# Moving transfers into neighbouring blocks, the projection into the int8 attention, and half of the value rounding to GpSimd

## What is computed

```python
def _layernorm(x, axis=-1, eps=1e-05):
    m = jnp.mean(x, axis=axis, keepdims=True)
    v = jnp.var(x, axis=axis, keepdims=True)
    return (x - m) / jnp.sqrt(v + eps)
...
def _L1_xattn_ref(x, cond, Wq, bq, Wkv, bkv, Wp, bp):   # H = 16 heads of hd = 32
    q = (x @ Wq + bq).reshape(1, B * N, H, hd)
    kv = (cond @ Wkv + bkv).reshape(1, -1, 2, H, hd)
    k, v = (kv[:, :, 0], kv[:, :, 1])
    ...
    q = _fq_sym(q, axis=-1)
    k = _fq_sym(k, axis=-1)
    v = _fq_sym(v, axis=2)
    attn = jnp.einsum('bhqd,bhkd->bhqk', q, k)
    attn = jax.nn.softmax(attn.astype(jnp.float32), axis=-1)
    attn = _fq_unsigned(attn, axis=-1)
    out = jnp.einsum('bhqk,bhkd->bhqd', attn, v)
    ...
    return out @ Wp + bp
```

## Time and profile before

| | us |
|---|---|
| median of three runs | 2641.4 (2641.16 to 2645.72) |
| profiled execution | 2642.37 |
| its span, first to last instruction | 2640.6 |
| granted TensorE clock, mean | 0.948 |

### The profile page before, as it was taken

How to read it: one execution, slowest core, us unless ns; L and a number is a source line. 1 busy time by engine, 2 the same in 40 slices (tenths; PEclk the granted TensorE clock), 3 DMA queues, 4 the chain that set the end, 5 groups by cost and what they waited for, 6 DMA issues and landing times. The chain is left out here.

```text
span 2640.6 us, 32466 instructions
## 1 busy us (share of the span) xinstructions
PE 2326.4 (88%) x11672; PEld 1586.5 (60%) x11672; DVE 1799.9 (68%) x3545; ACT 1252.7 (47%) x2207; POOL 503.7 (19%) x411
## 2 busy tenths in 40 slices
PE   3779999999999999967994988788888779999998
PEld 2556666666666665546772455545555437777776
DVE  7855777777777779776784966777777843464444
ACT  4443466666656666533442024676666853211111
POOL 7710033333333243420000011111101000000000
PEclk9879999999999999988997999999999969899999
DMA  3231100000010000024443000000000005456662
GB/s 133 107 135 36 36 17 29 8 29 28 13 32 9 29 9 13 0 80 183 168 144 137 0 21 10 1 10 1 6 5 1 1 20 196 180 219 230 224 226 75
DMA packets 47067, 184.89 MB, mean 70 GB/s; under 512 B 6272, under 2 KB 11136, under 8 KB 36672
## 3 DMA queue, kind: packets, MB, share of 16 engines
q1 hardware_dynamic: 46912, 182.86, 19.1%
HBM read 173.93 MB, written 8.91 MB: 69 GB/s over the span
## 5 line engine op out<-in xcount | busy, mean ns | idle before, releaser
L402 PE MATMUL wide_a<-wide_w,ctxT 128*128 128x256 f32 (+1 forms) x2048 | 436.1, 366 | 2.8 <-POOL wide_eps L371 2.8
L402 PEld LDWEIGHTS wide_a<-wide_w,ctxT 128*128 128x128 f32 x2048 | 367.0, 190 | 76.3 <-issue 35.7
L384 POOL TENSOR_TENSOR wide_sums<-wide_sums,wide_s 128x512 f32<-128x512 f32 x224 | 302.0, 1348 | 458.2 <-ACT wide_s L532 445.0
L1633 ACT ACTIVATE int_prob<-int_a,int_shift,int_qscale 128x512 uint8<-128x512 f32 x256 | 199.1, 786 | 103.5 <-PE int_a L1499 102.9
L427 PE MATMUL wide_scores<-wide_q,wide_keysT 128*128 128x512 f32 x512 | 238.4, 604 | 10.8 <-ACT wide_s L528 10.8
L437 PE MATMUL wide_o<-wide_s,wide_values 128*128 128x512 f32 x512 | 232.5, 597 | 3.5 <-ACT wide_s L532 3.5
L528 ACT COPY wide_s<-wide_scores 128x512 f32<-128x512 f32 x256 | 148.6, 586 | 180.0 <-PE wide_scores L427 168.6
L1753 DVE TENSOR_REDUCE int_peaks<-int_a 128x1 f32<-128x512 f32 x256 | 169.6, 685 | 60.0 <-PE int_a L1499 57.8
L1499 PE MATMUL int_a<-int_keys,int_qrows 96*128 96x512 bf16 x512 | 166.0, 408 | 41.8 <-DVE int_peaks L1753 34.8
L590 DVE TENSOR_TENSOR wide_top<-wide_top,wide_s 128x512 f32<-128x512 f32 x240 | 165.7, 691 | 15.4 <-ACT wide_s L528 9.6
L427 PEld LDWEIGHTS wide_scores<-wide_q,wide_keysT 128*128 128x128 f32 x512 | 87.9, 189 | 146.9 <-ACT wide_s L528 86.0
(11 more groups left out here) (416 smaller groups left out, 4277.1 us busy)
## 6 DMA issues: line engine op xcount, KB each, us to landing
moe_gate_up<-hbm_m_gu SPq DMA_DIRECT2D x34, 1408.0 KB, 6.2
moe_down<-hbm_m_down_a SPq DMA_DIRECT2D x34, 512.0 KB, 7.0
causal_wqkv<-hbm_wqkv SPq DMA_DIRECT2D x8, 1536.0 KB, 6.8
ctxT<-hbm_ctxT SPq DMA_DIRECT2D x4, 2048.0 KB, 14.8
oproj_raw<-hbm_wproj SPq DMA_DIRECT2D x8, 1024.0 KB, 5.3
ctxT_again<-hbm_ctxT SPq DMA_DIRECT2D x4, 2048.0 KB, 14.3
moe_down<-hbm_m_down_b SPq DMA_DIRECT2D x34, 192.0 KB, 7.3
wide_unit<-hbm_ffn_units SPq DMA_DIRECT2D x24, 256.0 KB, 2.6
```

The costliest lines, as they stand in the source:

```text
L384: ins = pool.tensor_tensor(sums[0][:, :], before, part[:, j, :], ALU.add)
L402: mm = pe.matmul(a[h][:, j, cols], ctxT[:, kc, t * P:(t + 1) * P], w[g % 2][:, kc, cols], start=(kc == 0), stop=(kc == KC - 1))
L1633: act.activation(prob[u % 4][:, j * 512:(j + 1) * 512], a[n % 4][:, :], ACT.Exp, bias=shift[:, u % NU:u % NU + 1], scale=qscale[:, t, h:h ...
```

## The change

- The layernorm before the FFN becomes part of the FFN's block (same instructions, without transposes and their copies), and `context_loads` are issued in that block.
- Two transfers of the causal stage and four of the decay stage move from the layernorm's block to the start of the next block. In the causal one they stand in front of the units' transfers in SyncE's queue.
- ScalarE takes one root of a constant ahead of the statistics in each layernorm, so the table is loaded then.
- The projection goes into the int8 stage. Its weights are loaded into the place of the query weights once the last values have been turned; TensorE runs its products right behind the last `finish`, those of the last chunk when VectorE has written its output; VectorE adds the bias ahead of the last `finish` and the products at the end.
- GpSimd rounds pieces 3 and 4 of each chunk, three instructions each; the pieces stand at steps 2, 6, 2 and 6. GpSimd now follows the common list, with its key instructions at their steps.
- In the last chunk VectorE casts six of eight turns of a head, before four.

```diff
@@ build_middle, ffn_stage, causal_attention_stage
-                    sp.dma_start(wqkv[1][:, :, :, :], A["wqkv0"][1]).then_inc(s_w[1], 16)
-                    sp.dma_start(wo[1][:, :, :], A["wo0"][1]).then_inc(s_wo[1], 16)
...
+                sp.dma_start(wqkv[1][:, :, :, :], A["wqkv0"][1]).then_inc(s_w[1], 16)
+                sp.dma_start(wo[1][:, :, :], A["wo0"][1]).then_inc(s_wo[1], 16)
                 for p in range(NP):
...
-            layernorm_stage(nc, "ln2", C, x, xT, xn=xn, loads=context_loads)
-            ffn_stage(nc, C, xn, weights, x)
+            ffn_stage(nc, C, x, weights, context_loads)
...
+            @block.sync
+            def _(sp):
+                loads(sp)
...
+                act.activation(std[:, NT:], eps[:, 0:1], ACT.Sqrt)
                 for t in range(NT):
...
+                    link(dve.bn_stats(stats[:, t, :], x[:, t, :]))
+                    dve.bn_aggr(mv[:, t, :], stats[:, t, :]).then_inc(s_var, 1)
+                for t in range(NT):
+                    dve.wait_ge(s_std, t + 1)
+                    link(dve.reciprocal(rstd[:, t:t + 1], std[:, t:t + 1]))
+                    link(dve.tensor_scalar(xn[:, t, :], x[:, t, :], mv[:, t, 0:1], rstd[:, t:t + 1], ALU.subtract, ALU.mult))
                     mx_dequantise(dve, link, xn[:, t, :], stat, power[:, :], shifted[:, :], deq[t][:, :]).then_inc(s_q, 1)
@@ int8_cross_attention_stage
-            return j % 2 == 0 and not (j % 4 == 2 and h % HC == HC - 1 and h // HC + 1 < CC)
+            if h // HC + 1 == CC:
+                return j % 4 != 3
+            return j % 2 == 0 and not (j % 4 == 2 and h % HC == HC - 1)
...
+                sp.wait_ge(s_b, use_b["value turned", CC - 1, 3] + 1)
+                sp.wait_ge(s_kp, CC * NS)
+                sp.dma_start(wp, A["x_wp"]).then_inc(s_wp, 16)
+                sp.dma_start(bp[:, :], A["x_bp"]).then_inc(s_wp, 16)
...
+                def round_values(c, piece):
+                    pool.wait_ge(s_vs, c + 1)
+                    cols = slice((piece - 1) * (SC // 4), piece * (SC // 4))
+                    if c >= 1:
+                        pool.wait_ge(s_b, use_b["value turned", c - 1, 3] + 1)
+                    pool.wait_ge(s_vc, c * NS + 2 * piece)
+                    link(pool.tensor_scalar(vT[:, cols], vT[:, cols], vstat[:, NS + 1:NS + 2], -127.0, ALU.mult, ALU.max))
+                    link(pool.tensor_scalar(vT[:, cols], vT[:, cols], ROUND_INT, ROUND_INT + 127.0, ALU.add, ALU.min))
+                    pool.tensor_scalar(vq[:, cols], vT[:, cols], ROUND_INT, None, ALU.subtract).then_inc(s_vp, 1)
+
+                for step in order:
+                    what, c, n = step
+                    if what == "key high":
+                        first_rest(c, n)
+                    elif what == "key middle":
+                        last_part(c, n)
+                    elif what == "value rounded" and n >= 3:
+                        round_values(c, n)
...
+                def project_out():
+                    pe.wait_ge(s_wp, 32)
...
+                    for c in range(CC):
+                        if c == CC - 1:
+                            pe.wait_ge(s_put, CC)
+                        for t in range(NT):
+                            mm = pe.matmul(a[t][:, :], outT[:, c, t * P:(t + 1) * P], wp[:, c, :], start=(c == 0), stop=(c == CC - 1))
...
+                        if x == CC - 1:
+                            dve.wait_ge(s_wp, 32)
+                            for t in range(NT):
+                                link(dve.tensor_tensor(residual[:, t, :], residual[:, t, :], bp[:, :], ALU.add))
                         finish(x)
...
+                    dve.wait_ge(s_xo, t + 1)
+                    dve.tensor_tensor(residual[:, t, :], residual[:, t, :], a[t][:, :], ALU.add)
@@ int8_order
-            place(base + max(4 * piece - 2, 0), "value rounded", c, piece)
+            place(base + (4 * ((piece - 1) % 2) + 2 if piece else 0), "value rounded", c, piece)
@@ build_last: of the loop over e the part for e = 1 moves into decay_attention_stage
+                sp.dma_start(wkv[1][:, :, :], A["d_wkv"][1]).then_inc(s_w[1], 16)
+                sp.dma_start(wq[1][:, :, :], A["d_wq"][1]).then_inc(s_w[1], 16)
+                sp.dma_start(decay[1][:, :, :, :], A["decay"][1]).then_inc(s_wo[1], 16)
+                sp.dma_start(wo[1][:, :, :], A["d_wo"][1]).then_inc(s_wo[1], 16)
```

More of the change, by code:

```diff
@@ L1040, in _, with ffn_stage @@
                     dve.tensor_tensor(x[:, t, :], x[:, t, :], acc[t][:, :], ALU.add)
-def ffn_stage(nc, C, xn, weights, x):
+def ffn_stage(nc, C, x, weights, loads):
     NF = 4
     with Stage(nc, "ffn") as st:
+        xn = st.sb("xn", [P, NT, DM])
+        stats = st.sb("stats", [P, NT, 6])
+        mv = st.sb("mv", [P, NT, 2])
+        eps = st.sb("eps", [P, 1])
+        std = st.sb("std", [P, NT + 1])
+        rstd = st.sb("rstd", [P, NT])
         deq = [st.sb(f"deq{e}", [P, DM]) for e in range(2)]
@@ L1087, in _ @@
             def _(act):
+                act.wait_ge(s_eps, 1)
+                act.activation(std[:, NT:], eps[:, 0:1], ACT.Sqrt)
+                for t in range(NT):
+                    act.wait_ge(s_var, t + 1)
+                    act.activation(std[:, t:t + 1], mv[:, t, 1:2], ACT.Sqrt, bias=eps[:, 0:1]).then_inc(s_std, 1)
                 for t in range(NT):
@@ L1468, in turn_values @@
                 def turn_values(c, m):
-                    pe.wait_ge(s_vq, 4 * c + m + 1)
+                    if m < 2:
+                        pe.wait_ge(s_vq, 2 * c + m + 1)
+                    else:
+                        pe.wait_ge(s_vp, 2 * c + m - 1)
                     e = use_b["value turned", c, m]
@@ L1568, in _ @@
                         finish(x)
+                project_out()
             @block.scalar
@@ L1738, in round_values @@
                         link(dve.tensor_scalar(s_v, peak_v, 1.0 / 127.0, 1e-8, ALU.mult, ALU.max))
-                        link(dve.reciprocal(inv_v, s_v))
+                        if c >= 1:
+                            dve.wait_ge(s_vp, 2 * c)
+                        dve.reciprocal(inv_v, s_v).then_inc(s_vs, 1)
+                        dve.wait_ge(s_vs, c + 1)
+                        return
+                    if piece >= 3:
                         return
@@ L1810, in _ @@
                     elif what == "finish":
+                        if x == CC - 1:
+                            dve.wait_ge(s_wp, 32)
+                            for t in range(NT):
+                                link(dve.tensor_tensor(residual[:, t, :], residual[:, t, :], bp[:, :], ALU.add))
                         finish(x)
-def projection_stage(nc, name, zT, n_in, w_dram, bias_dram, x):
-    with Stage(nc, name) as st:
-        w = st.sb("w", [P, n_in, DM])
-        bias = st.sb("bias", [P, DM])
-        acc = [st.ps(f"acc{t}", [P, DM]) for t in range(NT)]
-        s_in, s_mm, s_dve = (st.sem(n) for n in ("loaded", "products", "dve"))
-        with nc.Block() as block:
-            @block.sync
-            def _(sp):
-                sp.dma_start(w[:, :, :], w_dram).then_inc(s_in, 16)
-                sp.dma_start(bias[:, :], bias_dram).then_inc(s_in, 16)
-            @block.tensor
-            def _(pe):
-                pe.wait_ge(s_in, 32)
-                for t in range(NT):
-                    for j in range(n_in):
-                        mm = pe.matmul(acc[t][:, :], zT[:, j, t * P:(t + 1) * P], w[:, j, :], start=(j == 0), stop=(j == n_in - 1))
-                    mm.then_inc(s_mm, 1)
-            @block.vector
-            def _(dve):
-                link = Chain(dve, s_dve).after
-                dve.wait_ge(s_in, 32)
-                for t in range(NT):
-                    link(dve.tensor_tensor(x[:, t, :], x[:, t, :], bias[:, :], ALU.add))
-                    dve.wait_ge(s_mm, t + 1)
-                    link(dve.tensor_tensor(x[:, t, :], x[:, t, :], acc[t][:, :], ALU.add))
+                for t in range(NT):
+                    dve.wait_ge(s_xo, t + 1)
+                    dve.tensor_tensor(residual[:, t, :], residual[:, t, :], a[t][:, :], ALU.add)
 def build_int8_attention(nc, C, A, x, context):
```

64 lines of the change are left out of this document (35 added, 29 removed).

## The result

| kernel | median of its runs, us | ratio to before, 95% interval |
|---|---|---|
| before | 2641.9 (2641.16 to 2645.72) | |
| after | 2602.2 (2596.01 to 2610.53) | 0.985 (0.982 to 0.988) |

A forecast was written before the change was run, and what follows sets the result against it. Bound: a row of stages with all-engine barriers between; no engine full in int8 chunk 0. Sum from 2642.4: -17.5 - 0.4 - 7.5 + 9.6 + 6.4 + 0.5 = -8.9, 2633.5, forecast 2633 us; own range 2622 to 2636, eight in ten 2612 to 2652.

The forecast's parts named there:

- FFN's seam: Between causal stage and FFN: with the layernorm inside the FFN's block only SyncE waits for its 12.97 us issue; 17.5 us gained.
- Causal seam: Before the causal stage: two transfers moved to the next block shorten VectorE's wait; 0.4 us gained, bounds 0 and 0.9.
- Projection: After attention: 12 of 16 matmul passes run straight behind the last sums; 7.5 us gained after 0.3 for bias additions.
- six slow passes: In the projection after attention: six matmul passes at 0.85 us, as before, and six at 0.43, 7.7 us together.
- The pieces on GpSimd: Int8 stage, value rounding moved off VectorE: a loss of 9.6 us in chunks 0 to 2 and 6.4 in chunk 3.
- VectorE's way to SBUF: Int8 stage: GpSimd's instructions, 3.0 us each, block VectorE's SBUF access; about 10.8 us standing still in a chunk's first 25.
- my walk through the earlier trace: Chunk 0 with GpSimd and VectorE taking alternating turns: VectorE's piece instructions take 1.8 to 2.9 us, 10.8 us standing in all.
- a lock over the whole instruction: SBUF access: an exclusive lock held for the whole instruction by VectorE's two-port modes and its instructions with two SBUF inputs.
- The 45% passed on: Int8 stage: 45% of VectorE's 10.8 us standing lengthens a chunk, 4.8 us, bounds 0 and all of it.
- the 1.6 us for the pieces removed: Int8 stage: two pieces fewer on VectorE gain 0.6 and 1.0 us, 1.6 us a chunk.
- Casts in the last chunk: VectorE takes 24 of 32 casts instead of 16: middle nothing, near the end -1.9, after the exponentials +1.0; +0.5 us in all.
- the first, 2615: GpSimd is cheap, 1.05 to 1.5 us an instruction; int8 gain and loss cancel, only the seams count: 2615 us, chance 0.22.

The follow-up runs named there:

- 2591.0 us kernel: The changed kernel with the last chunk's casts as before and each piece of values rounded in two instructions instead of three, on both engines: 2591.0 us (0.981).

## Why the prediction was wrong, point by point

By the medians the 30.7 us between forecast and result divide so: 16.5 for a cost of the int8 stage that didn't come, some 9 that the int8 loop gained, by the experiments through the key order, which I had not costed, and 5.5 for the seams, which brought 30.9 where I had 25.4.

- **FFN's seam**, -17.5: right (-17.9 at the first reduction and -17.1 at the stage's end in the profile; 18.1 us earlier and 20.6 in the median where it was made alone). A further 2.6 us came ahead of the int8 loop at a higher clock, which I had not; 1.2 of them came also where nothing ahead was changed.
- **Causal seam**, -0.4: it can't be told. The end of that stage is 0.6 us earlier after, but 3.2 earlier in the kernel with the projection's merge alone, which changes nothing ahead of it, and between 7.0 earlier and 5.3 later in kernels that share the causal edit.
- **Projection**, -7.5: right in kind, low by 1.6 (-9.1), inside its bounds. I had six slow passes; there were about four, which is 0.8 of the 1.6. The bias additions, charged with 0.3, cost nothing: with the old casts the tail is 14.1 us with and without them.
- **The pieces on GpSimd**, +16.0: wrong. This is the step that failed: its size is off in both of its factors (1 and 2), and beside it an effect of the same rewritten loop was left out (3).
  1. *The step "VectorE's way to SBUF"*. GpSimd's instructions were longer than I assumed, 3.7, 3.8 and 2.9 us instead of 3.0:

```profile
L1419 POOL TENSOR_SCALAR int_vT<-int_vT,int_vstat x8: 3707/3712/4043, 1610.5 to 2043.4; 128x1024 f32<-128x1024 f32 x8
L1420 POOL TENSOR_SCALAR int_vT<-int_vT x8: 3636/3794/3962, 1614.3 to 2047.5; 128x1024 f32<-128x1024 f32 x8
L1421 POOL TENSOR_SCALAR int_vq<-int_vT x8: 2777/2870/3201, 1618.4 to 2051.3; 128x1024 bf16<-128x1024 f32 x8
```

     VectorE's lines beside them, of after, should by my walk through the earlier trace rows have shown 2 to 3.5 us, and show their usual 0.7 or at most 0.8 us more:

```profile
L1818 DVE TENSOR_SCALAR int_vT<-int_vT,int_vstat x8: 742/800/1352, 1615.2 to 2043.0; 128x1024 f32<-128x1024 f32 x8
L1819 DVE TENSOR_SCALAR int_vT<-int_vT x8: 693/694/1481, 1616.0 to 2043.9; 128x1024 f32<-128x1024 f32 x8
L1820 DVE TENSOR_SCALAR int_vq<-int_vT x8: 694/1401/1410, 1616.7 to 2045.4; 128x1024 bf16<-128x1024 f32 x8
```

     Adding up what every VectorE instruction took over its usual time, VectorE stood 3.2, 3.3, 2.0 and 2.0 us in chunks 0 to 3, not 10.8. Against that, the 1.4 us a chunk that it had stood before in steps 35 to 42 are gone. The earlier trace rows had misled me, since GpSimd's instructions there are 1.2 and 1.7 us long: one can't see in them whether VectorE waits for the end or for a part. The Trainium skill, "SBUF — State Buffer", section "Who interferes with whom", which I had cited for a lock over the whole instruction, doesn't fit these rows: VectorE's pieces took at most 0.8 us more beside GpSimd instructions of 2.8 to 4.0 us.
  2. *The 45% passed on, and the 1.6 us for the pieces removed.* With 2 x 2.13 us less work and 2 to 3.3 us of standing, VectorE is left with 1 to 2 us less a chunk, and steps 0 to 15 went from 122.2 us (all on VectorE, new key order) to 120.5. That difference is inside what such kernels differ by: seven of them with all pieces on VectorE at the same steps have 117.9 to 122.2. Its two halves are clearer: steps 0 to 11, where GpSimd works beside VectorE, took 4.6 us more (84.1 to 88.7) although one of VectorE's pieces left them, and steps 12 to 15, which lost their piece, 6.3 less (38.1 to 31.8). So both effects of the forecast are there, the loss far smaller and the gain larger. Where the standing was nearly gone, two pieces of 1.4 us off VectorE gave 1.6 a chunk, and four instructions of 0.69 less on VectorE (2.8 us) shortened the same steps from 122.2 to 112.2, 3.3 a chunk. So 45% was too low for steps 0 to 15, and it did little harm because the amount it was applied to was far too high. The 1.6 us for the pieces I had read in chunk 0 alone; the same comparison in chunks 1 and 2 of before gives 4.0 (7.9 and 13.4 us for 6.5 and 10.8), and it isn't a clean one, since steps 8 to 11 of these chunks take 7.9 also without a piece (2591.0 us kernel).
  3. *What was left out*: the order of the key steps in the same rewritten GpSimd loop, 11.3 us by itself (2630.9 against 2642.2) and 9.6 beside the merged seams (2601.7 against 2611.3). I had asked only whether the turning of the values waits for GpSimd, and not what else stands in its queue. It was to be seen before: TensorE's key turns named GpSimd as releaser for 3.8 us, and GpSimd's last part started the instant the next tile's rest ended. The wait itself is small: in steps 32 to 35, at a clock of 1.00 in both kernels, it is 10.3 us before and 9.9 after. Most of the gain goes with the clock, which was 0.80 to 0.95 before in seven of the nine four-step stretches from 36 on, and 1.00 after in all nine. That the waits pull the clock down is argued, not shown; with the new order in the kernel before it was 1.00 in six of the nine.
- **Casts in the last chunk**, +0.5, of which +1.0 in the tail: the tail is right (+1.0), and so is the gain near the end (-1.8 for -1.9); the middle, and so the sum, can't be told from nothing.
- **Rivals.** The nearest was the first, 2615, with the opposite reason: GpSimd was not cheap (2.8 to 4.0 us an instruction), it was harmless. Its consequence was right, VectorE standing some 3 us a chunk and gain and loss cancelling, its condition wrong. The observations that I named against the forecast came in part: VectorE's lines stayed near 0.7 or took 0.8 more at most, and GpSimd's were not near 1. The first 12 steps of a chunk were 0.7, 2.4, 4.1 and 1.6 us longer than before, where I had named 4 to 8. The 1.8 cycles an element of the Trainium skill, "GPSIMD Engine Reference", section "Performance versus the Vector engine", from which I had an estimate of 1.5 us at most, is given there as a best case, so it was no ceiling. My smallest time, 2612, was too high since no case had a gain in the loop.

## What to carry to other kernels

When a diff rewrites the loop of an engine to add something, list everything the new loop issues in another order; here that side effect was worth 9 to 11 us, and the thing that was meant added nothing measurable. A short wait of TensorE for a lightly used engine (busy 9 of 43 us here) is worth undoing, since a lower clock can go with it. Ahead of giving work to GpSimd, choose its operations: with multiply and add, a tile of 128x1024 took 1.05 us, with a maximum or minimum 3.6 or more; and leaving out two comparisons that change no value (the factor is 127 over the peak) brought 10 to 14 us by the medians, wherever the pieces lay, the best kernel here being 2587.9 us against 2641.9 and 2602.2.

## What the runs showed of the hardware

- GpSimd's tensor_scalar of 128x1024 f32: 1.05 us for multiply and add (also into bf16, and 1.12 with the factor from a tile), 2.78 for subtract alone, 3.63 for multiply and maximum and, at the least, for add and minimum. VectorE takes 0.69 to 0.74 for each of the piece's three.
- VectorE beside GpSimd: an instruction that reads and writes SBUF was held up by 0.95 us at most (0.68 to 1.63, beside a GpSimd instruction of 1.15), and by 0.84 and 0.86 whether GpSimd's had 3.6 or 1 us left; three in a row ran at full speed beside one of 3.96 us (VectorE from 1615.19 to 1617.39, GpSimd's L1420 from 1614.32). That one was itself longer than the 3.64 us which the same line took elsewhere, so the delay can fall on GpSimd's side.
- The granted clock of a stretch changed with small edits elsewhere, and gave or took 1.5 us in four steps (9.26 us at 1.00 or 10.72 at 0.85 for the same steps 36 to 39). Runs of one kernel scattered by up to 18 us, so a gain under some 4 us needs the profile's stretches beside the median.
